# Graph layers with attention and FFN: load order, VectorE order, and who splits the weights

## The reference, cut to what matters

```python
for l in range(3):
    si = x @ attn_w[l, :d]; sj = x @ attn_w[l, d:]
    scores = si[:, :, None] + sj[:, None, :] + attn_b[l]
    scores = jnp.where(scores >= 0, scores, 0.2 * scores)
    scores = jnp.where(mask, scores, -jnp.inf)
    attn = jax.nn.softmax(scores, axis=-1)
    agg = jnp.einsum('bij,bjd->bid', attn, x)
    h = layernorm(x + agg, g1[l], beta1[l])
    ff = jax.nn.gelu(h @ W1[l] + b1[l], approximate=False) @ W2[l] + b2[l]
    x = layernorm(h + ff, g2[l], beta2[l])
```

## Time and profile before

| what | value |
|---|---|
| median of 3 executions | 1868.31 us (1865.25 to 1874.41) |
| the profiled execution, its own time | 1871.55 us |
| its span, first to last instruction | 1869.6 us |
| TensorE matmul, busy | 1670.7 us (89%) |
| VectorE, busy | 1379.5 us (74%) |
| GpSimd, busy | 1269.8 us (68%) |
| ScalarE, busy | 1206.6 us (65%) |
| mean granted TensorE clock | 0.959 of full speed |

### The profile page before, as it was taken

One profiled execution on the slowest core, in us unless ns is written; L12 is line 12 of the kernel. 1 busy time (PEld: TensorE's weight loads), 2 busy tenths in 40 slices (PEclk: granted clock), 3 DMA queues, 4 the chain that ended last, 5 costly groups with the idle time before them and its releaser, 6 DMA issues.

```text
span 1869.6 us, 40745 instructions
## 1 busy us (share of the span) xinstructions
PE 1670.7 (89%) x12032; PEld 1475.7 (79%) x12032; DVE 1379.5 (74%) x5414; ACT 1206.6 (65%) x2814; POOL 1269.8 (68%) x2260
## 2 busy tenths in 40 slices
PE   5999999974999999998899999999988999999995
PEld 4777877863888888888788888888877888887894
DVE  2888888887776777667766776677676887777873
ACT  3888888873665666656555666666656666666662
POOL 3255555533676766767566866766767999998996
PEclk8999999995999999999989999999999999999997
DMA  6222232332211212212131211212211222122111
GB/s 183 63 89 81 84 90 90 90 97 85 74 49 52 67 34 67 61 40 68 34 97 49 67 46 55 67 34 67 67 34 57 68 68 90 59 76 73 66 42 45
DMA packets 152115, 127.39 MB, mean 68 GB/s; under 512 B 16512, under 2 KB 145024, under 8 KB 152064
## 3 DMA queue, kind: packets, MB, share of 16 engines
q1 hardware_dynamic: 145024, 124.30, 21.6%
q10 hardware_dynamic: 7040, 2.51, 0.5%
HBM read 89.04 MB, written 37.75 MB: 68 GB/s over the span
## 4 chain that ended last, share of the span: by engine, by line
PE 28%; POOL 17%; DVE 9%; issue 8%; DMA 7%; SPq 4%; ACT 3%; POOLq 0%; ACTq 0%; DVEq 0%
PE ps L834 13%; PE ps L45 10%; DMA ab<-in_L_gnn_attn_b 7%; POOL xo L772 5%; POOL gnn_norm L766 4%; POOL gnn_norm L156 4%; DVE gnn_junk L940 3%; PE ps L821 3%; POOL inv L151 2%; DVE gnn_st L1007 2%; DVE gnn_res L1003 2%; PE ps L807 2%; SPq L124 1%; SPq L126 1%; SPq L689 1%
## 5 line engine op out<-in xcount | busy, mean ns | idle before, releaser
L834 PE MATMUL ps<-gnn_w_hi,gnn_g_hi 128*128 128x256 f32 x1536 | 446.6, 291 | 70.7 <-DVE gnn_res L1003 70.5
L834 PE MATMUL ps<-gnn_w_lo,gnn_g_hi 128*128 128x256 f32 x1536 | 435.6, 284 | 0.0
L834 PE MATMUL ps<-gnn_w_hi,gnn_g_lo 128*128 128x256 f32 x1536 | 435.3, 283 | 0.0
L143 POOL TENSOR_TENSOR fence_pool<-half_neg 128x1 f32<-128x1 f32 x346 | 65.8, 199 | 501.4 <-DVE gnn_mv L1101 235.3
L917 ACT ACTIVATE gnn_g_hi<-ps,b_cols 128x512 fp32r<-128x512 f32 x384 | 264.6, 689 | 211.8 <-PE ps L45 211.7
L1011 DVE TENSOR_TENSOR gnn_g_lo<-ps,gnn_g_hi 128x512 fp32r<-128x512 f32 x384 | 263.0, 685 | 161.7 <-ACT ps L918 161.6
L834 PEld LDWEIGHTS ps<-gnn_w_hi,gnn_g_hi 128*128 128x128 f32 x1536 | 296.0, 193 | 81.3 <-DVE gnn_res L1003 78.8
L45 PE MATMUL ps<-gnn_hT_hi,gnn_w_hi 128*128 128x512 f32 x768 | 341.1, 444 | 3.9 <-DVE gnn_g_lo L1011 3.9
L45 PE MATMUL ps<-gnn_hT_lo,gnn_w_hi 128*128 128x512 f32 x768 | 305.6, 398 | 0.0
L45 PE MATMUL ps<-gnn_hT_hi,gnn_w_lo 128*128 128x512 f32 x768 | 305.5, 398 | 0.0
L940 DVE CUSTOM_DVE_ANT_0 gnn_junk<-x,aw 128x256 f32<-128x256 f32 x384 | 213.1, 600 | 120.6 <-DMA ab<-in_L_gnn_attn_b 120.1
(11 more groups left out here) (120 smaller groups left out, 3882.5 us busy)
## 6 DMA issues: line engine op xcount, KB each, us to landing
hist<-xo SPq DMA_DIRECT2D x48, 512.0 KB, 3.3
x<-hist SPq DMA_DIRECT2D x48, 512.0 KB, 4.2
gmask<-mask_hist SPq DMA_DIRECT2D x48, 256.0 KB, 4.2
aw<-in_L_gnn_attn_w SPq DMA_DIRECT2D x48, 256.0 KB, 4.1
att_xq<-in_x SPq DMA_DIRECT2D x16, 512.0 KB, 4.6
att_xl<-in_x SPq DMA_DIRECT2D x16, 512.0 KB, 3.6
gnn_fin<-hist SPq DMA_DIRECT2D x16, 512.0 KB, 3.9
out<-gnn_fin SPq DMA_DIRECT2D x16, 512.0 KB, 3.0
```

The lines of the kernel that those rows point to most:

```text
L834: mm = e.matmul(FF2[j % 2], g[a][:, m, j * N:(j + 1) * N], V[b][:, m, :], start=(n == 0), stop=(n == len(terms) - 1))
```

## The change

1. SyncE issues the loads of the next step ahead of the store of this one, in the first two layers. The weights of the next layer are loaded after the first pair of steps (w1) and after the second (w2), no longer ahead of both.
2. Within a load, the attention vectors come right behind x; bias and mask follow and have a semaphore of their own (`m_ld`), which `masked_sums` waits for.
3. VectorE's order: residual 0, `probs_max`, residual 1, sums 0 and 1, residual 2, `hT_lo`, sums 2 and 3, statistics.
4. Weight splits: the high part of w1 is made by ScalarE (`split_w1_hi`), between the exponentials and `hT`; its low part stays with VectorE. The high part of w2 stays with VectorE, its low part goes half to VectorE and half to GpSimd (`split_w2_lo`, ahead of `ln_ffn`). For this ScalarE's and GpSimd's loops are cut at the last pair of a layer.
5. GpSimd's fence ahead of each norm's first instruction becomes a plain wait, and that instruction adds `eps` as a tensor. The fence further on in the norm stays.

```diff
-            e.tensor_scalar(inv[:, 0, :], stats[:, :, 1], EPS, None, ALU.add).then_inc(chain, 1)
+            e.tensor_tensor(inv[:, 0, :], stats[:, :, 1], eps[:], ALU.add).then_inc(chain, 1)
...
+                def pair_of_steps(q):
+                    load_ahead(q, 1)
+                    store_x(q, 0)
+                    load_ahead(q + 1, 0)
+                    store_x(q, 1)
+
+                load_ahead(0, 0)
                 with e.Fori(0, L - 1) as l:
-                    e.wait_ge(w_split, 2 * (l + 1))
-                    load_layer_weights(e, l + 1)
-                    with e.Fori(0, pairs) as p:
-                        for par in range(2):
-                            load_ahead(l * pairs + p, par)
-                            store_x(l * pairs + p, par)
+                    pair_of_steps(l * pairs)
+                    e.wait_ge(w1_split, 2 * (l + 1))
+                    load_w1(e, l + 1)
+                    pair_of_steps(l * pairs + 1)
+                    e.wait_ge(w2_split, 2 * (l + 1))
+                    load_w2(e, l + 1)
+                    with e.Fori(2, pairs) as p:
+                        pair_of_steps(l * pairs + p)
...
-                    hold_pool(e, mv1_out, t1 + 1)
                     if not isinstance(t1, int):
-                        hold_pool(e, hT_made, 2 * t1)
+                        e.wait_ge(hT_made, 2 * t1)
+                    e.wait_ge(mv1_out, t1 + 1)
...
+                def split_w2_lo(l):
+                    e.wait_ge(w2_hi_set, l + 1)
+                    for m in range(FT // 2):
+                        ins = e.tensor_tensor(V[1][:, m, :], w2_raw[:, m, :], V[0][:, m, :].bitcast(F32), ALU.subtract)
+                    ins.then_inc(w2_split, 1)
...
+                    if layer_end:
+                        split_w2_lo(layer_of(2 * q + par + 1))
                     ln_ffn(2 * q + par, par, q, final or isinstance(q, int))
...
+                def split_w1_hi(l):
+                    e.wait_ge(w_ld, 32 * (l + 1))
+                    for k in range(KT):
+                        e.copy(W[0][:, k, :], w1_raw[:, k, :]).then_inc(w1_hi_set, 1)
...
                     if more >= 2:
                         exps(t + 2)
+                    if layer_end:
+                        split_w1_hi(layer_of(t + 1))
...
-                    if more >= 3:
-                        attention_sums(t3, p3, h3, 0)
                     residual2(t, par, 0)
                     if more >= 2:
                         probs_max(t2)
                     if final:
                         final_sum(q, par)
-                    if layer_end:
-                        split_w1(layer_of(t1), 0)
-                    if more >= 3:
-                        attention_sums(t3, p3, h3, 1)
                     residual2(t, par, 1)
                     if layer_end:
-                        split_w1(layer_of(t1), 1)
+                        split_w1_lo(layer_of(t1), 0)
                     if final:
                         final_statistics(q, par)
                     if more >= 3:
+                        attention_sums(t3, p3, h3, 0)
+                        attention_sums(t3, p3, h3, 1)
+                    residual2(t, par, 2)
+                    if layer_end:
+                        split_w1_lo(layer_of(t1), 1)
+                    if more >= 1:
+                        hT_lo(t1)
+                    if more >= 3:
                         attention_sums(t3, p3, h3, 2)
                         attention_sums(t3, p3, h3, 3)
-                    residual2(t, par, 2)
-                    if layer_end:
-                        split_w1(layer_of(t1), 2)
-                        split_w1(layer_of(t1), 3)
-                    if more >= 1:
-                        hT_lo(t1)
...
-                    e.tensor_copy(V[0][:], w2_raw[:]).then_inc(w_hi_set, 1)
-                    e.wait_ge(w_hi_set, 3 * l + 3)
-                    e.tensor_tensor(V[1][:], w2_raw[:], V[0][:].bitcast(F32), ALU.subtract).then_inc(w_split, 1)
+                    e.tensor_copy(V[0][:], w2_raw[:]).then_inc(w2_hi_set, 1)
+                    e.wait_ge(w2_hi_set, l + 1)
+                    e.tensor_tensor(V[1][:, FT // 2:FT, :], w2_raw[:, FT // 2:FT, :], V[0][:, FT // 2:FT, :].bitcast(F32),
+                                    ALU.subtract).then_inc(w2_split, 1)
```

More of the change, by code:

```diff
@@ L95, in gnn_kernel @@
         half_neg = sb("half_neg", [P, GROUP])
+        eps = sb("eps", [P, GROUP])
         w1_raw = sb("w1_raw", [P, KT, F])
@@ L109, in gnn_kernel @@
         g_ld = sems("g_ld_even", "g_ld_odd")
+        m_ld = sems("m_ld_even", "m_ld_odd")
         mask1_st = sems("mask1_st_even", "mask1_st_odd")
@@ L114, in gnn_kernel, with load_w1, load_w2 @@
         stored = sems("stored_even", "stored_odd")
-        def load_layer_weights(e, layer):
+        def load_w1(e, layer):
             e.dma_start(w1_raw[:], W1[bass.ds(layer, 1)].rearrange("o (k p) f -> p (o k) f", p=P)).then_inc(w_ld, 16)
+        def load_w2(e, layer):
             e.dma_start(w2_raw[:], W2[bass.ds(layer, 1)].rearrange("o (m p) d -> p (o m) d", p=P)).then_inc(w_ld, 16)
@@ L248, in _ @@
                 e.dma_start(xq[:], block_of(x_g, 1)).then_inc(xq_ld, 16)
-                load_layer_weights(e, 0)
+                load_w1(e, 0)
+                load_w2(e, 0)
                 def body(q, par, more):
@@ L283, in _ @@
                                 pattern=[[-1, P]], channel_multiplier=1).then_inc(ident_set, 1)
+                e.memset(eps[:], EPS)
                 e.memset(half_neg[:], -0.5).then_inc(eye_made, 1)
@@ L787, in body @@
                         final_norm(t1, p1)
+                    if layer_end:
+                        split_w2_lo(layer_of(2 * q + par + 1))
                     ln_ffn(2 * q + par, par, q, final or isinstance(q, int))
                 ln_attention(0, 0)
-                steps(e, body, peel_last_layer=True)
+                split_w2_lo(0)
+                steps(e, body, peel_layer_end=True, peel_last_layer=True)
                 final_norm(T - 1, 1)
@@ L924, in body @@
                             gelu_table(1)
+                split_w1_hi(0)
                 exps(0)
@@ L929, in _ @@
                 hT_hi(0)
-                steps(e, body)
+                steps(e, body, peel_layer_end=True)
             @block.vector
@@ L944, in attention_sums, with masked_sums @@
                         ins.then_inc(aij_out, 1)
-                def masked_sums(t2, par2):
+                def masked_sums(t2, par2, half2):
+                    e.wait_ge(m_ld[par2], 32 * (half2 + 1))
                     hold_dve(e, sjT_made, t2 + 1)
@@ L1036, in final_statistics, with split_w1_lo @@
                     ins.then_inc(mv3_out, 1)
-                def split_w1(l, n):
-                    k = n % 2
-                    if n < 2:
-                        if n == 0:
-                            e.wait_ge(w_ld, 32 * (l + 1))
-                        e.tensor_copy(W[0][:, k, :], w1_raw[:, k, :]).then_inc(w_hi_set, 1)
-                    else:
-                        e.wait_ge(w_hi_set, 3 * l + k + 1)
-                        ins = e.tensor_tensor(W[1][:, k, :], w1_raw[:, k, :], W[0][:, k, :].bitcast(F32), ALU.subtract)
-                        if n == 3:
-                            ins.then_inc(w_split, 1)
+                def split_w1_lo(l, k):
+                    e.wait_ge(w1_hi_set, KT * l + k + 1)
+                    e.tensor_tensor(W[1][:, k, :], w1_raw[:, k, :], W[0][:, k, :].bitcast(F32), ALU.subtract).then_inc(w1_split, 1)
                 def body(q, par, more, layer_end, final):
@@ L1053, in body @@
                     t1, p1, _ = ahead(q, par, 1)
-                    t2, p2, _ = ahead(q, par, 2)
+                    t2, p2, h2 = ahead(q, par, 2)
                     t3, p3, h3 = ahead(q, par, 3)
@@ L1114, in _ @@
                     attention_sums(0, 0, 0, j)
-                masked_sums(0, 0)
+                masked_sums(0, 0, 0)
                 attention_shifts(0, 0)
-                split_w1(0, 0)
-                split_w1(0, 1)
                 probs_max(0)
-                split_w1(0, 2)
-                split_w1(0, 3)
+                split_w1_lo(0, 0)
+                split_w1_lo(0, 1)
                 for j in range(GROUP):
@@ L1127, in _ @@
                     attention_sums(1, 1, 0, j)
-                masked_sums(1, 1)
+                masked_sums(1, 1, 0)
                 attention_shifts(1, 1)
```

23 lines of the change are left out of this document (11 added, 12 removed).

## The result

The changed kernel takes 1767.57 us (median of 4 executions, 1766.54 to 1768.08) against 1867.66 us for the kernel before (4 executions, 1865.25 to 1874.41). The ratio is 0.946, with a 95% interval of 0.943 to 0.948: 100 us less. The forecast was 1766.

The account below looks back on a forecast made before the run. TensorE's own work was the floor, 26.0 us a step, with a stop per step above it. Savings of 82 + 13 + 6 + 1 = 102 us off 1871.55 gave 1769.5, about 1766 against the median; range 1742 to 1814.

Parts of the forecast that it names:

- The stop and its cause: First two layers: TensorE stops 1.8 us per step for VectorE's residual, held by late loads and sums ahead of it.
- Inner steps, 82 us: 28 inner steps of the first two layers: 26.0 us each, 728 instead of 810.5 us, saving 82.
- The clock: First two layers: half-clock dips, about 36 us in all, follow the stops and go in the 28 inner steps.
- the clock doesn't come back: Rival, chance 0.10: stops go, but 36 us of clock loss stay because dips have another cause; 1799 us.
- GpSimd closes a loop: Rival, chance 0.03: GpSimd's loop, put at 23.5 us, stretches and sets steps of 29.5 us; 1885 us.
- VectorE becomes the bound: Rival, chance 0.13: longer VectorE sums or ScalarE high parts make `hT_lo` 1.1 us late each inner step; 1797 us.
- Borders, 13 us: Four steps at the two layer borders: 123 us instead of 135.8, saving 13; bounds 0 and 25.
- The zero for four more gaps: Borders: cutting ScalarE's and GpSimd's loops might add four gaps of 2.7 us, 11 us; taken as zero.
- the `g_lo` stop: A layer's first step: TensorE's stop of 3.6 us for `g_lo` was forecast to stay.
- Last layer, 6 us: 13 last-layer steps: 0.5 us saved per step, 6 us; bounds 4 us lost and 21 us saved.
- the last layer gains in full: Rival, chance 0.12: last-layer sums run beside an idle GpSimd, or borders gain fully; 15 to 25 us more, 1745.
- The step that failed: the fences: GpSimd's removed fences: all beside TensorE except three at the very end, 0.8 us; `eps` as a tensor taken as zero.

Follow-up runs that it names:

- a1: The kernel before with SyncE's new order alone (loads ahead of stores, w1 and w2 loaded after the first and second pair): 1784.49 us, ratio 0.956.
- a2: The kernel before with VectorE's new order alone, loads still behind stores and weight splits where they were: 1787.59 us, ratio 0.958.
- d1: The changed kernel with SyncE's old order (loads behind stores, w1 and w2 loaded at a layer's start): 1774.28 us, ratio 0.948.
- d2: The changed kernel with VectorE's old order (sums 0 ahead of residual 0, `hT_lo` last): 1779.81 us, ratio 0.952.
- a3: The kernel before with only GpSimd's fences removed and `eps` added as a tensor: 1840.54 us, ratio 0.986.
- b4: The changed kernel with two more unread sum instructions ahead of residual 2 in the first two layers: 1801.00 us, ratio 0.967.
- b3: The changed kernel with all weight splits back on VectorE and ScalarE's and GpSimd's loops not cut: 1770.09 us, ratio 0.950.
- c1: The changed kernel with all of GpSimd's old fences and the constant `eps` back in every norm: 1768.72 us, ratio 0.949.
- b1: The changed kernel with the attention stage's norm wholly as before (fence and constant `eps`): 1757.39 us, ratio 0.944 to the kernel before.
- b5: b1 with all four sums behind `hT_lo` in the last layer: 1739.46 us, ratio 0.934 to the kernel before.
- a4: The changed kernel with only the fence of the attention stage's norm put back, `eps` still a tensor: 1762.89 us, ratio 0.944.
- c2: b5 with one fence more in the attention stage's norm: 1739.93 us, ratio 0.933 to the kernel before.

## Why the prediction was right, and where it was not

**The stop and its cause: right.** It named one stop per step, in front of the FFN's second half, and said that both the late load and the place of the sums made it. a1 and a2 show that mending one of the two is enough to remove this stop, though `hT_lo` then comes a few tenths late; d1 and d2 show what each is worth once the other is in: 6.7 and 12.2 us. The loads' share is not in the inner steps but mostly at the first border.

**Inner steps, 82 us: 85.5 measured.** The step's own time table held within 0.3 us at each place read above. The floor of 26.0 us, TensorE's matmuls without a hole, came out as 25.9, and its own rows say so: 48 matmuls at 0.117 and 8 transposes in 0.9 are 6.5 us and not 6.6.

**The clock: right.** The dips of the inner steps went with the stops, and the rival "the clock doesn't come back" (1799) fell. a3 says more. Over the 32 steps its stops are 1.8 us on average, borders included, and 27 of the 28 inner steps ran at 1.00; before, with 2.2 on average, 13 of the 28 had fallen. (The rival's 1799 adds 33 us for the 36 named beside it, which makes no difference here.)

**A rival that was priced wrong.** "GpSimd closes a loop" was put at 1885 us, with 42 us for 28 steps of 29.5. The inner step before is 810.5 / 28 = 28.95 us, so such steps cost 15 us more, and with 20 saved elsewhere the rival comes to about 1864: no slower than before. It did not happen.

**"VectorE becomes the bound": not so in the inner steps, but near.** b4 puts the cover at 0.6 us where 0.9 was taken; beyond it VectorE does set the step.

**Borders, 13 us: 18.5 measured.** The zero for four more gaps was right (the one gap on VectorE, 2.64 us, is the old one). ScalarE's cast was cheap, as forecast: two in 2.00 us, and then ScalarE still waited 0.60 us for the transposes. GpSimd's half was mis-sized, 3.84 us where 3.2 stood. The two rows, from the timelines at the first border:

```profile
877.39 2.00 ACT L934 CAST gnn_w_hi<-w_raw 128x1024 fp32r<-128x1024 f32 x2
```

```profile
893.81 3.84 POOL L794 TENSOR_TENSOR gnn_w_lo<-w_raw,gnn_w_hi 128x256 fp32r<-128x256 f32 x4 [10.48 <-DVE gnn_w_hi L1127]
```

VectorE's half of the low part starts at 893.76, just ahead of it, and takes 1.23 us. Four GpSimd additions or products of the same shape, with VectorE otherwise busy, take 2.83 us a little later, so some 1.0 us of the 3.84 came from standing beside VectorE:

```profile
901.88 2.83 POOL L781 TENSOR_TENSOR gnn_norm<-gnn_norm,affine 128x256 f32<-128x256 f32 x4 [0.18 <-POOL gnn_norm L160]
```

By the Trainium skill ("SBUF — State Buffer", Who interferes with whom) the two halves would stand one behind the other, and the prediction put that at 1.2 us. The trace's 1.0 us agrees here, and it is GpSimd that paid. `n1` was late by 0.67 us at 913.48 (forecast 1.5) and by 1.88 at the second border, and the `g_lo` stop stayed with 3.39 us. But by b3 the splits were worth 2 us in all. Half of the 18.5 is TensorE's busy time, which fell by 5.75 and 3.43 us at the two borders with the clock (0.88 before and 0.97 after at the first, 0.95 and 1.00 at the second), where the forecast had counted half of the first border's loss; most of the rest are the stops.

**Last layer, 6 us: 11.1 measured.** The step for the order of the sums was small, as said; what was left out is the fences. c1 against b1 puts them at 7.2 us in these 13 steps, 6.4 of them as TensorE's busy time with the clock (0.98 against 1.00). The wait for `hT_lo` stayed, as forecast; the changed kernel's rows for the 13 steps (the ones without a releaser stand at the same place):

```profile
PE ps L823 <- issue: 10.8, 7, 1.6
PE ps L823 <- DVE gnn_hT_lo L1048: 8.0, 5, 1.8
```

b5 shows that the rival "the last layer gains in full" was there to be had, but not by this change: two of the sums stood ahead of `hT_lo`.

**The step that failed: the fences.** They were put down as "all beside TensorE", with the addition of `eps` "taken as zero". In the inner steps that held, and at the very end they gave 0.9 us for the forecast 0.8. Elsewhere in the layers they were worth more than that (about 11 us: 7.2 in the last layer and 3.7 ahead of it, nearly all at the borders), and in the attention stage, which the forecast called "not where the change works", the same edit cost 10.2 us (b1). The two nearly cancel (c1), which is why the sum didn't show it.

What happens there can be read in VectorE's groups between 205 and 350 us (busy, mean ns). Before, the change, and the same after it:

```profile
L559 DVE TENSOR_TENSOR att_attT_lo<-att_att,att_attT_hi 128x256 fp32r<-128x256 f32 x24 | 10.2, 426 | 0.8
...
L557 DVE CAST att_attT_hi<-att_att 128x256 fp32r<-128x256 f32 x24 | 7.1, 294 | 0.8
...
L524 DVE TENSOR_SCALAR att_neg_peak<-att_peak 128x8 f32<-128x8 f32 x24 | 4.1, 169 | 0.2
```

```profile
L565 DVE TENSOR_TENSOR att_attT_lo<-att_att,att_attT_hi 128x256 fp32r<-128x256 f32 x23 | 12.0, 522 | 0.8
...
L563 DVE CAST att_attT_hi<-att_att 128x256 fp32r<-128x256 f32 x23 | 8.4, 365 | 0.8
...
L530 DVE TENSOR_SCALAR att_neg_peak<-att_peak 128x8 f32<-128x8 f32 x24 | 7.6, 319 | 0.2
```

The instructions are the same, and 96, 71 and 150 ns longer on average. Only some of them are: 6 of the 23 low parts take 0.8 us, 6 of the 23 casts 0.4 to 0.7, and 12 of the 24 short ones 0.45 to 0.50, each of them beside a GpSimd instruction; the rest are as before. In b1 they are back at 425, 294 and 179. Both a long cast of the changed kernel and a short one of before start inside the same GpSimd operation; what differs is how far into it (1.36 and 0.66 us). GpSimd and VectorE in the changed kernel, then in the kernel before:

```profile
295.13 1.94 POOL L298 TENSOR_SCALAR att_mask<-att_adjl 128x512 f32<-128x512 int32 x1
...
296.49 0.73 DVE L563 CAST att_attT_hi<-att_att 128x256 fp32r<-128x256 f32 x1
```

```profile
289.76 1.94 POOL L292 TENSOR_SCALAR att_mask<-att_adjl 128x512 f32<-128x512 int32 x1
...
290.42 0.30 DVE L557 CAST att_attT_hi<-att_att 128x256 fp32r<-128x256 f32 x1
```

This is no chance pair. In the 14 traces 316 casts of this line start inside one of GpSimd's operations on the mask, about 1.94 us long. The 222 that start up to 1.34 us into it take 0.29 to 0.43 us. Of the 94 that start at 1.35 or later, 93 end 0.14 or 0.15 us behind GpSimd's end, however late they start. One run, a4, has both kinds:

```profile
267.18 1.94 POOL L298 TENSOR_SCALAR att_mask<-att_adjl 128x512 f32<-128x512 int32 x1
...
268.54 0.73 DVE L563 CAST att_attT_hi<-att_att 128x256 fp32r<-128x256 f32 x1
```

```profile
292.76 1.95 POOL L298 TENSOR_SCALAR att_mask<-att_adjl 128x512 f32<-128x512 int32 x1
...
293.78 0.30 DVE L563 CAST att_attT_hi<-att_att 128x256 fp32r<-128x256 f32 x1
```

None of the late starts is in a kernel with the old norm in this stage or in c2, 14 or 15 are in each kernel with the changed one, and 9 in a4.

The Trainium skill ("SBUF — State Buffer", Who interferes with whom) says that a VectorE cast and a GpSimd operation can exclude each other for a whole instruction. The late casts agree with it. The early ones do not: the one of before at 290.42 ends at 290.72 while GpSimd's operation, which had begun first, runs to 291.70.

So the cause is shown as far as the edit (the fence and `eps` in that norm), its size and the instructions that it lengthens, and for the casts the phase between GpSimd and VectorE is what decides. a4 (half back) and b1 (all back) fit. c2 does not follow from it: its useless fence gains 1.6 us more, but the three groups take 425, 307 and 210 ns there, no less than in b1. Why the last 0.6 us of GpSimd's operation are dear and the rest is not, and why kernels with the same stage spread from 431.2 to 435.4, stays open.

## What to carry to other kernels

Before costing an edit at nothing because its engine has time, list every stage that calls the edited helper: here one function serves four norms, and a fence of 0.17 us less and another form of one small addition gave 11 us in one place and took 10 in another. When several parts of a change attack one stop, price them in sequence, since each alone may remove it, and read what bounds next. Put work that nobody waits for behind the instruction that the bounding engine waits for: in the last layer that order alone was worth 18 us.

## What the runs showed of the hardware

- TensorE's granted clock in steps with a stop each: 0.99 over 911.5 us with stops of 1.8 us on average (a3), 0.96 over 946.3 us with 2.2 on average. Less than half a microsecond per stop went with some 20 us.
- A VectorE cast beside a 1.94 us GpSimd operation: unhurt when it starts up to 1.34 us into it (222 casts, 0.29 to 0.43 us), held to 0.15 us past its end when it starts at 1.35 or later (93 of 94).
- A VectorE operation of 8 columns that is 0.17 us long on average before is 0.32 after, with the same operands: half of them take 0.45 to 0.50, all of these beside a GpSimd instruction.
- VectorE waits 2.64 us without a releaser ahead of line 1127, at the first border, and not at the second; it was 2.66 before. With ScalarE's and GpSimd's loops cut in the same way, the waits of those two in the changed kernel list no such gap at the borders; GpSimd stands there for 10.48 us waiting for VectorE, so one could be hidden.
